# Three edits around two gathered matrix products: slots found in batches, turned tiles copied by ScalarE, stores issued by SyncE

## The chip, the core and the metric

The kernel runs on one NeuronCore of a Trainium2 chip. The metric is device time in microseconds, lower is better. Before the change the median of three runs is 1250.01 us (1247.91 to 1253.24).

## What is computed

32 images of 3x96x96 are cut into 16x16 patches, shifted and embedded (36 tokens of 192 numbers each), and 32 text tokens are fetched from a table. That gives T = 2176 tokens, 17 tiles of 128. One attention layer of 12 heads, which keeps the 32 largest scores, is added to them. What matters here is the last layer, cut to its core:

```python
x = layernorm(h)                                  # [2176, 192]
logits_fk = (x @ W_fk + b_fk) @ normed(emb_fk).T  # [2176, 128], the same for rk
w_fk, _ = topk_sparsify(softmax(logits_fk), 4)    # 4 of 128 weights stay, made to sum to 1
w_rk, _ = topk_sparsify(softmax(logits_rk), 4)
all_h = einsum('bsd,ndr->bsnr', x, f_know)        # f_know: 128 matrices of 192x128
h1 = einsum('bsnr,bsn->bsr', all_h, w_fk)
all_out = einsum('bsr,nrd->bsnd', h1, r_know)     # r_know: 128 matrices of 128x192
h = h + einsum('bsnd,bsn->bsd', all_out, w_rk)
```

Only the products with a weight are made: 4 for each token and each of the two layers.

## The kernel before

Up to 526 us the kernel embeds and attends; up to 615 us it chooses four matrices for each token (routing). Neither is touched. Then, all in f32:

- *Slots.* Each (token, matrix) pair gets a row, a slot, in a DRAM buffer in which the rows of one matrix lie together. `find_slots(r, i)` on VectorE (L1481) works the slots of tile i for layer r out in six short dependent steps, four comparisons against a list of the 128 matrices among them. For r = 0 all 17 tiles are done in a row; then the weights are made to sum to 1 (`weights_known`), and `m_xT`, which lies over the same memory as the positions of r = 0, is cleared (L1525).
- *Scatter.* GpSimd sends each tile's rows to their slots with four indirect DMAs (L692, buffer `slots_x`). The tokens are split into part 0 (tiles 0 to 8) and part 1 (9 to 16); `sent0` and `sent1` count the landed ones.
- *First product.* A part is a list of groups of 4 x 128 slots: 25 groups in part 0, 24 in part 1. 16 of each are main groups, in which every half tile of 64 slots belongs to a fixed matrix; the others are spill groups, whose matrix numbers are read at run time. Part 0 has the spill groups last, part 1 has them first. For a group SyncE loads 384 KB of rows (`load_rows`, L456), up to four groups ahead; TensorE turns each tile (L1152, a transpose into PSUM); VectorE copies the turned tile from PSUM to `m_halves` (`turned_first`, L1534); TensorE multiplies (L1166 main, L1163 spill); ScalarE copies the product from PSUM to `m_yh` (`keep_first`, L886) and issues the store of the group to `slots_h` on its own DMA queue. TensorE turns two tiles ahead of the two that it multiplies. `m_yh` has four buffers (`m_out0` to `m_out3` count their stores).
- *Sums.* When all stores of a part have landed, GpSimd fetches for each of its tiles the four product rows of each token (`fetch`, L700), VectorE finds the tile's slots of layer r = 1 and adds the rows, weighted (`first_sums`: `find_slots` and `sum_back`, L1559, L1562), and GpSimd scatters the sums into `slots_g` (`spread_sums`, L707).
- *Second product.* The same with 256 KB loads (L498), L1201 for turning, `turned_second` (L1542) for VectorE's copy, L1212 and L1210 for main and spill, `keep_second` (L903) and 384 KB stores. `r_know` (16 chunks of 768 KB) is loaded over `f_know` in part 1 of the first product, each chunk as soon as the matrices beneath it have had their last use.
- *Output.* GpSimd fetches the rows of `slots_y`, VectorE adds them and the residual (L1571), SyncE stores them (L487).

Each engine runs its own list in order. VectorE's list is written out by `beside`: all the turned copies of part 0; then those of part 1 with the nine `first_sums` of part 0 between them, one after every two or three groups; then the turned copies of the second product with the `first_sums` of part 1 and the output sums of part 0 between them. SyncE's list holds the loads, `load_r`, and later the output stores; before its first `load_rows` it waits for `slots_zeroed`, `weights_known`, `tiles_known`, issues the last three chunks of `f_know`, and waits for `sent0`.

## Time and profile before

| what | us |
|---|---|
| median of three runs | 1250.01 |
| the profiled execution | 1248.79 |
| its span, first to last instruction | 1247.0 |
| TensorE busy with matmuls | 881.7 (71%) |
| VectorE busy | 753.1 (60%) |
| GpSimd busy | 529.8 (42%) |
| ScalarE busy | 329.2 (26%) |
| mean granted TensorE clock | 0.742 of full speed |

The profile comes from one execution with the hardware profiler; its times run from the first instruction. L1152 is line 1152 of the kernel. Busy shares are means over stages of quite different limits, so the stages are read one by one. In a row, out<-in names the tiles with buffer numbers left out; some names stand for the memory they lie in: `early` holds the loaded rows and the gathered rows and sums, `place` holds `m_halves`, `m_y` also `m_yh`. "idle before <-releaser" is the engine's idle time before that instruction and what ended it, as inferred from semaphore events; "remote" is a release for which the profile shows no source.

### The profile page before, as it was taken

How to read it: one execution, taken by the hardware profiler on the slowest of the kernel's cores; microseconds unless marked ns; L12 is line 12 of the kernel's file. 1: busy time of each engine (PE TensorE's matmuls, PEld its weight loads, DVE VectorE, ACT ScalarE, POOL GpSimd, SP SyncE). 2: the span in 40 equal slices, each digit the busy share in tenths (PEclk: the TensorE clock that was granted, in tenths of full speed). 3: DMA queues.
4: the chain of work that ended last, by engine and by line, in shares of the span. 5: the costliest groups of instructions: out<-in, count | busy, mean ns of one | idle time of the engine just before them, and what ended most of it. 6: DMA issues, size and time to landing. Idle time of an engine off the chain costs nothing.

```text
span 1247.0 us, 24432 instructions
## 1 busy us (share of the span) xinstructions
PE 881.7 (71%) x6616; PEld 750.0 (60%) x6616; DVE 753.1 (60%) x4773; ACT 329.2 (26%) x1042; POOL 529.8 (42%) x745
## 2 busy tenths in 40 slices
PE   4788988898989898667400099987778656757830
PEld 4788878888888787444200088987556333633630
DVE  1399999999999999444553444334445344424533
ACT  0234433333433343144200033211111222213410
POOL 3244444444544443245376500043443544454235
PEclk9778888787878655555555599987775676878975
DMA  5123332323233330086021555444785544447833
GB/s 189 33 69 110 141 110 89 109 89 109 90 109 111 113 113 25 19 208 162 7 79 67 169 196 188 149 126 126 256 318 205 182 146 151 140 154 229 272 127 95
DMA packets 81318, 167.70 MB, mean 134 GB/s; under 512 B 12944, under 2 KB 39376, under 8 KB 79536
## 3 DMA queue, kind: packets, MB, share of 16 engines
q1 hardware_dynamic: 55824, 111.18, 27.5%
q10 hardware_dynamic: 14112, 32.12, 7.4%
q0 software_dynamic: 11264, 23.09, 6.3%
q8 instruction: 42, 0.69, 0.2%
q14 instruction: 76, 0.62, 0.2%
HBM read 84.81 MB, written 81.53 MB: 133 GB/s over the span
## 4 chain that ended last, share of the span: by engine, by line
PE 36%; DVE 32%; issue 18%; POOL 5%; DMA 4%; another core or an unknown queue 2%; ACT 2%; DVEq 1%; SPq 0%; POOLq 0%; ACTq 0%
DVE work L1301 13%; DVE top L1295 9%; PE bank L1166 6%; PE bank L1163 5%; PE bank L1212 5%; PE bank L1152 4%; PE bank L1210 3%; POOL early L700 2%; PE bank L1201 2%; PE bank L1099 1%; PE bank L925 1%; PE bank L984 1%; PE bank L1006 1%; POOL slots_g L707 1%
## 5 line engine op out<-in xcount | busy, mean ns | idle before, releaser
L1301 DVE MATCH_REPLACE8 work<-top,work 102x68 f32<-102x68 f32 x1024 | 204.7, 212 | 0.0
L1534 DVE COPY place<-bank 96x256 f32<-96x256 f32 x196 | 74.5, 416 | 149.2 <-PE bank L1152 98.3
L1295 DVE MAX8 top<-work 102x8 f32<-102x68 f32 x1024 | 145.5, 213 | 3.2 <-ACT tru L767 1.9
L1152 PE MATMUL bank<-ident,early 128*96 128x128 f32 x392 | 73.4, 316 | 102.9 <-DMA early<-slots_x 101.2
L886 ACT ACTIVATE m_y<-bank 128x128 f32<-128x128 f32 x196 | 52.5, 278 | 304.2 <-PE bank L1166 207.9
L1542 DVE COPY place<-bank 128x128 f32<-128x128 f32 x196 | 47.5, 286 | 133.0 <-PE bank L1201 73.1
L707 POOL DMA_INDIRECT slots_g<-early,s_all x68 | 66.1, 973 | 138.8 <-DVE early L1562 123.2
L1152 PEld LDWEIGHTS bank<-ident,early 128*96 128x96 f32 x392 | 52.3, 175 | 118.3 <-issue 117.9
L700 POOL DMA_INDIRECT early<-slots_h,s_all x68 | 65.2, 959 | 122.9 <-DMA slots_h<-m_y 102.5
L925 PE MATMUL bank<-xa,early 128*96 128x144 f32 x512 | 102.0, 352 | 16.8 <-DVE early L1319 16.0
L903 ACT ACTIVATE m_y<-bank 128x192 f32<-128x192 f32 x196 | 61.1, 331 | 170.5 <-PE bank L1212 78.8
L1166 PE MATMUL bank<-f_all,place 96*64 96x128 f32 x1024 | 92.6, 324 | 15.0 <-issue 11.1
L925 PEld LDWEIGHTS bank<-xa,early 128*96 128x96 f32 x512 | 91.5, 200 | 18.2 <-issue 15.9
L1212 PE MATMUL bank<-r_all,place 128*64 128x192 f32 x512 | 70.3, 400 | 40.5 <-DVE place L1542 25.6
L700 POOL DMA_INDIRECT early<-slots_y,s_all x68 | 64.7, 952 | 68.8 <-DMA slots_y<-m_y 29.9
L1166 PEld LDWEIGHTS bank<-f_all,place 96*64 96x64 f32 x1024 | 71.9, 160 | 30.2 <-issue 18.2
L1006 PE MATMUL bank<-v,pT 68*68 68x17 f32 x768 | 75.9, 250 | 14.6 <-ACT pT L792 14.6
L1006 PEld LDWEIGHTS bank<-v,pT 68*68 68x68 f32 x768 | 74.0, 196 | 17.1 <-ACT pT L792 17.1
L692 POOL DMA_INDIRECT slots_x<-early,s_all x68 | 66.0, 970 | 40.8 <-DVE s_all L1506 20.6
L1163 PE MATMUL bank<-f_all,place 96*128 x544 | 73.5, 293 | 10.5 <-ACT m_y L886 4.3
L629 POOL TENSOR_TENSOR sc<-work,tru 102x544 f32<-102x544 f32 x32 | 42.7, 1333 | 90.0 <-ACT work L805 89.9
L1301 DVE MATCH_VALUE_LOAD work<-top,work 102x8 f32 x1024 | 80.2, 78 | 0.0
(179 smaller groups left out, 1815.9 us busy)
## 6 DMA issues: line engine op xcount, KB each, us to landing
early<-slots_x SPq DMA_DIRECT2D x49, 384.0 KB
slots_y<-m_y ACTq DMA_DIRECT2D x49, 384.0 KB
slots_h<-m_y ACTq DMA_DIRECT2D x49, 256.0 KB
early<-slots_g SPq DMA_DIRECT2D x49, 256.0 KB
f_all<-in_f_know SPq DMA_DIRECT2D x16, 768.0 KB, 5.6
r_all<-in_r_know SPq DMA_DIRECT2D x16, 768.0 KB
slots_x<-zero SPq DMA_DIRECT2D x28, 360.0 KB, 3.0
slots_x<-zero SPq DMA_DIRECT2D x28, 336.0 KB, 3.2
```

The source lines that it names most:

```text
L692: nc.gpsimd.indirect_dma_start(slots_x[part_of(i)], bass.IndirectOffsetOnAxis(s_all[:, 0, i, k:k + 1], 0), xn_all[:, i, :], None).then_inc ...
L700: nc.gpsimd.indirect_dma_start(g_in[:, i % DEPTH, k, 0:width], None, src, bass.IndirectOffsetOnAxis(s_all[:, r - 1, i, k:k + 1], 0)).then_ ...
L707: nc.gpsimd.indirect_dma_start(slots_g[part_of(i)], bass.IndirectOffsetOnAxis(s_all[:, 1, i, k:k + 1], 0), g_sum[:, i % DEPTH, 0:R], None) ...
L925: nc.tensor.matmul(half, wa[:, 4 * a + c, e * HALF:(e + 1) * HALF], xa[:, :, a:a + 2 * GRID - 1:2, c:c + 2 * GRID - 1:2], start=(a == 0 an ...
L1006: last = nc.tensor.matmul(ps_pt[0:S, head * (HD + 1):(head + 1) * (HD + 1)], pT[:, g, h * S:(h + 1) * S], v[:, par, head, :], start=True, ...
L1152: last = nc.tensor.transpose(turn_bank[t][0:HALF, c * P:(c + 1) * P], m_x[:, d, t, c:D:2], ident[:])
L1163: last = nc.tensor.matmul(bank[2 + t][:, 0:R], m_xT[0:HALF, t, c, h * P:(h + 1) * P], matrix[:, c * R:(c + 1) * R], start=(h == 0 and c == ...
L1166: last = nc.tensor.matmul(bank[2 + t][h * HALVED:(h + 1) * HALVED, 0:R], m_halves[0:HALF, t, c, h, :], matrix[:, c * R:(c + 1) * R], start ...
L1212: last = nc.tensor.matmul(bank[2 + t][h * HALVED:(h + 1) * HALVED, 0:D], m_halves[:, t, 0, h, :], matrix, start=True, stop=True)
L1295: last = nc.vector.max(top8[:, c, :], work[:, par, c, :])
L1301: last = nc.vector.match_replace(work[:, par, c, :], top8[:, c, :], work[:, par, c, :], TAKEN)
L1534: nc.vector.tensor_copy(m_halves[0:HALF, t], turn_bank[t][0:HALF, 0:2 * P].rearrange("p (c h s) -> p c h s", c=2, h=2)).then_inc(sem["m_xt ...
```

## The change

`find_slots` takes a batch of tiles at a time, in four batches (1, 2, 6 and 8 tiles), and both layers are done before any product; the weights come after the second batch. The turned tiles are copied by ScalarE, two tiles ahead of the products that it keeps, and VectorE has only the sums after the slots. The stores of both products are issued by SyncE, one after each `load_rows` or `load_sums` of its loop.

```diff
+BATCHES = ((0, 1), (1, 3), (3, 9), (9, NT))
+IN_FLIGHT = 8
...
+            def store_rows(r, g, n, rows, at, copies):
+                j = FIRST_GROUP[g] + n
+                sp.wait_ge(sem[f"m_done{r}"], (j + 1) * GROUP)
+                sp.dma_start(rows[at * GROUP * P:(at + 1) * GROUP * P, :].rearrange("(p t) d -> p t d", p=P),
+                             copies[:, j % DEPTH]).then_inc(sem[f"m_out{j % DEPTH}"], 16)
...
                     if n + DEPTH < PART_GROUPS[g]:
                         load_rows(g, n + DEPTH)
+                    store_rows(0, g, n, slots_h[g], first_order(g)[n], m_yh)
                     while g == 1 and chunk < CHUNKS and n > PART_GROUPS[1] - PART_MAIN + ...
                         load_r(chunk)
...
                     if n + DEPTH < PART_GROUPS[g]:
                         load_sums(g, n + DEPTH)
+                    store_rows(1, g, n, slots_y[g], n, m_y)
...
-                pool.wait_ge(sem["slots_known0"], i + 1)
+                pool.wait_ge(sem["slots_known0"], 1 + [i < end for first, end in BATCHES].index(True))
...
             def spread_sums(i):
                 pool.wait_ge(sem["summed1"], i + 1)
+                pool.wait_ge(sem["slots_known1"], 1 + [i < end for first, end in BATCHES].index(True))
...
-            def keep_first(g, n):   (and keep_second: both wait, copy and issue the store)
+            def copy_turned(r, j, t):
+                act.wait_ge(sem[f"m_turn{r}"], j * GROUP + t + 1)
+                if j >= 1:
+                    act.wait_ge(sem[f"m_mm{r}"], (j - 1) * GROUP + t + 1)
+                if r == 0:
+                    ins = nc.scalar.activation(m_halves[0:HALF, t], turn_bank[t][0:HALF, 0:2 * P]..., ACT.Copy)
+                else:
+                    ins = nc.scalar.activation(m_halves[:, t, 0], turn_bank[t][:, 0:P]..., ACT.Copy)
+                ins.then_inc(sem[f"m_xt{r}"], 1)
+
+            def keep(r, g, n, copies, width):
+                j = FIRST_GROUP[g] + n
+                d = j % DEPTH
+                for t in range(0, GROUP, AHEAD):
+                    for ahead in range(t + AHEAD, t + 2 * AHEAD):
+                        if ahead < GROUP:
+                            copy_turned(r, j, ahead)
+                        elif n + 1 < PART_GROUPS[g]:
+                            copy_turned(r, j + 1, ahead - GROUP)
+                    if t == 0 and r * GROUPS + j >= DEPTH:
+                        act.wait_ge(sem[f"m_out{d}"], 16 * (in_turn(d, GROUPS) * r + j // DEPTH))
+                    for now in range(t, t + AHEAD):
+                        act.wait_ge(sem[f"m_mm{r}"], j * GROUP + now + 1)
+                        nc.scalar.activation(copies[:, d, now, :], bank[2 + now][:, 0:width], ACT.Copy).then_inc(sem[f"m_done{r}"], 1)
...
+                for m in range(size * K4):
+                    i, k = divmod(m, K4)
+                    if m >= IN_FLIGHT:
+                        st.wait(IN_FLIGHT - 1)
+                    st.done(nc.vector.scalar_tensor_tensor(s_hit[:, m % IN_FLIGHT], iota_e[:], ids[:, i, k:k + 1], here[:, i],
+                                                           ALU.is_equal, ALU.mult, accum_out=s_f[:, i, k:k + 1]))
...
+            find_slots(0, 0)
+            find_slots(0, 1)
+            spread_weights()
+            for n in range(2, len(BATCHES)):
+                find_slots(0, n)
             nc.vector.memset(m_xT, 0.0).then_inc(sem["halves_cleared"], 1)
+            for n in range(len(BATCHES)):
+                find_slots(1, n)
...
-            def beside(turned, g, tiles, step):   (and turned_first, turned_second)
+            for i in range(NT):
                 sum_back(1, i, R)
+            for i in range(NT):
                 sum_back(2, i, D)
```

In the batched `find_slots` the other steps stand once for the whole batch, over [128, tiles, 128] or [128, tiles, 4].

## Rows read from the trace of the kernel before

**Rows 1.** Busy time of each engine by stage.
```profile
core 0: us, PE busy (x) PEld busy (x) DVE busy (x) ACT busy (x) POOL busy (x), PEclk, DMA share, GB/s
615.00:716.00 101.00, 0.04 (x1) 0.00 (x0) 47.85 (x278) 0.00 (x0) 65.96 (x68) 0.50 0.29 95
716.00:815.00 99.00, 98.77 (x1025) 88.30 (x1026) 39.08 (x104) 28.05 (x101) 0.00 (x0) 0.98 0.56 180
815.00:966.00 151.00, 122.28 (x937) 101.21 (x935) 69.03 (x272) 24.50 (x95) 66.03 (x69) 0.75 0.61 207
...
975.00:1105.00 130.00, 87.03 (x500) 59.07 (x499) 54.32 (x260) 31.59 (x100) 57.49 (x61) 0.78 0.49 153
```

**Rows 2.** In order of time (start, length, engine, line), from scatters to first turn.
```profile
619.30 1.19 POOL L692 DMA_INDIRECT slots_x<-early,s_all  x1 [13.11 <-DVE s_all L1506]
...
664.03 0.96 POOL L692 DMA_INDIRECT slots_x<-early,s_all  x1 [0.30 <-issue]
...
703.25 1.76 DVE L1525 MEMSET place<- 128x2048 f32 x1 [0.60 <-DVE weights L1521]
704.04 25.42 SPq L456 DMA_DIRECT2D early<-slots_x  x8
...
716.23 1.93 PE L1152 MATMUL bank<-ident,early 128*96 128x128 f32 x8 [101.19 <-DMA early<-slots_x]
```

**Rows 3.** In order of time, VectorE: first step of tiles 0 and 1, a late step.
```profile
615.67 0.29 DVE L1488 SCALAR_TENSOR_TENSOR s_over<-place,base 128x128 f32<-128x128 f32 x1 [0.15 <-DVE tile_e L1475]
...
618.47 0.29 DVE L1488 SCALAR_TENSOR_TENSOR s_over<-place,base 128x128 f32<-128x128 f32 x1
...
663.67 0.16 DVE L1497 SCALAR_TENSOR_TENSOR s_i<-idf,s_f 128x4 int32<-128x4 f32 x1 [8.34 <-remote]
```

**Rows 4.** In order of time, TensorE in both products, undisturbed.
```profile
726.73 0.69 PE L1152 MATMUL bank<-ident,early 128*96 128x128 f32 x4
...
728.42 0.68 PE L1152 MATMUL bank<-ident,early 128*96 128x128 f32 x4
...
1149.09 0.44 PE L1201 MATMUL bank<-ident,early 128*128 128x128 f32 x2
...
1150.26 0.44 PE L1201 MATMUL bank<-ident,early 128*128 128x128 f32 x2
...
1188.73 1.47 PE L1210 MATMUL bank<-r_all,place 128*128 x8
```

**Rows 5.** The chain that ended last (start, length, link), spill groups of part 0.
```profile
775.24 1.79 PE bank L1163 x16
777.47 1.79 PE bank L1163 x16
```

**Rows 6.** In order of time, ScalarE: a 96x256 copy in the routing.
```profile
551.17 0.38 ACT L841 ACTIVATE t_xT<-bank 96x256 f32<-96x256 f32 x1
```

**Rows 7.** The page's costliest groups: ScalarE's copies of the products.
```profile
L886 ACT ACTIVATE m_y<-bank 128x128 f32<-128x128 f32 x196 | 52.5, 278 | 304.2 <-PE bank L1166 207.9
...
L903 ACT ACTIVATE m_y<-bank 128x192 f32<-128x192 f32 x196 | 61.1, 331 | 170.5 <-PE bank L1212 78.8
```

**Rows 8.** VectorE's turned copies (L1534, L1542), by stretches with GpSimd active: busy, count, clock, DMA.
```profile
815.40:825.40 10.00, 1.95 (x5) 1.00 0.40 120
...
905.40:915.40 10.00, 2.71 (x8) 0.95 0.92 345
...
1022.90:1032.80 9.90, 2.04 (x9) 0.79 0.37 113
...
1110.00:1126.00 16.00, 2.21 (x9) 0.71 0.57 179
```

**Rows 9.** In order of time: loads to first turn in the second product, last store.
```profile
971.90 4.34 SPq L498 DMA_DIRECT2D early<-slots_g  x5
...
974.80 1.09 PE L1201 MATMUL bank<-ident,early 128*128 128x128 f32 x4 [10.28 <-DMA early<-slots_g]
...
1196.46 0.33 ACTq L905 DMA_DIRECT2D slots_y<-m_y  x1
```

More of the change, by code:

```diff
@@ L320, in wait, with __init__, done @@
                 self.eng.wait_ge(self.sem, self.base + self.at)
+        class Tally:
+            def __init__(self, eng, name):
+                self.eng, self.sem, self.count = eng, sem[name], 0
+            def done(self, ins):
+                ins.then_inc(self.sem, 1)
+                self.count += 1
+            def wait(self, lag=0):
+                self.eng.wait_ge(self.sem, self.count - lag)
         def logits_of(i):
@@ L908, in _ @@
+            act.wait_ge(sem["m_mm0"], GROUPS * GROUP)
             for g in range(2):
-                for j in range(FIRST_GROUP[g], FIRST_GROUP[g] + PART_GROUPS[g]):
-                    keep_second(g, j)
+                for t in range(AHEAD):
+                    copy_turned(1, FIRST_GROUP[g], t)
+                for n in range(PART_GROUPS[g]):
+                    keep(1, g, n, m_y, D)
         @block.tensor
@@ L1477, in _, with find_slots @@
             nc.vector.sem_inc(sem["tiles_known"], 1)
-            slot_steps = [Steps(dve, f"slot_steps{r}", 6) for r in range(2)]
-            def find_slots(r, i):
-                st = slot_steps[r]
-                q, size = 2 * part_of(i) + r, HALVED
-                st.start(i)
-                st.done(nc.vector.scalar_tensor_tensor(s_over[:], place[:, r, i], float(size), base[:, q], ALU.is_ge, ALU.mult))
+            slot_steps = Tally(dve, "slot_steps")
+            def find_slots(r, n):
+                st = slot_steps
+                first, end = BATCHES[n]
+                size = end - first
+                here = place[:, r, first:end]
+                ids = idf[:, first:end, r]
+                starts = base[:, 2 * part_of(first) + r].unsqueeze(1).to_broadcast([P, size, NE])
+                st.done(nc.vector.scalar_tensor_tensor(s_hit[:, 0:size], here, float(HALVED), starts, ALU.is_ge, ALU.mult))
@@ L1489, in find_slots @@
                 st.wait()
-                st.done(nc.vector.tensor_tensor(s_at[:], s_over[:], place[:, r, i], ALU.add))
+                st.done(nc.vector.tensor_tensor(here, s_hit[:, 0:size], here, ALU.add))
                 st.wait()
-                for k in range(K4):
-                    last = nc.vector.scalar_tensor_tensor(s_hit[:, k, :], iota_e[:], idf[:, i, r, k:k + 1], s_at[:],
-                                                          ALU.is_equal, ALU.mult, accum_out=s_f[:, k:k + 1])
@@ L1495, in find_slots @@
-                st.done(last)
+                for m in range(size * K4):
[4 more added lines that the diff above has]
+                                                           ALU.is_equal, ALU.mult, accum_out=s_f[:, i, k:k + 1]))
                 st.wait()
-                st.done(nc.vector.scalar_tensor_tensor(s_i[:, 0], idf[:, i, r], float(size), s_f[:], ALU.mult, ALU.add))
+                at = [s_i[:, step, 0:size] for step in range(4)]
@@ L1571, in sum_back @@
                     nc.vector.tensor_tensor(g_sum[:, d, :], g_sum[:, d, :], t_h[:, i % 2, :], ALU.add).then_inc(sem["summed2"], 1)
-            def first_sums(i):
-                find_slots(1, i)
+            for i in range(NT):
                 sum_back(1, i, R)
-            def beside(turned, g, tiles, step):
-                done = 0
-                for n in range(PART_GROUPS[g]):
-                    turned(FIRST_GROUP[g] + n)
-                    while done < len(tiles) and (done + 1) * PART_GROUPS[g] <= (n + 1) * len(tiles):
-                        step(tiles[done])
-                        done += 1
-                assert done == len(tiles)
-            def output(i):
-                sum_back(2, i, D)
-            for n in range(PART_GROUPS[0]):
-                turned_first(n)
-            beside(turned_first, 1, range(*PARTS[0]), first_sums)
-            dve.wait_ge(sem["m_mm0"], GROUPS * GROUP)
-            beside(turned_second, 0, range(*PARTS[1]), first_sums)
-            beside(turned_second, 1, range(*PARTS[0]), output)
-            for i in range(*PARTS[1]):
-                output(i)
+            for i in range(NT):
+                sum_back(2, i, D)
 _INS = ["a_x", "l_x", "text_ids", "w_shift_a", "w_shift_l", "w_mid_a", "w_mid_l", "tok_vec", "tok_bias", "vocab",
```

89 lines of the change are left out of this document (29 added, 60 removed).

## The prediction

> **What bounds the kernel now.** I read the busy time by stage first, then the start of the dispatch in order of time, then the rhythm of the two products with and without GpSimd beside them. The changed code runs after 615 us; what lies before it is untouched. The stages [rows 1] say three things. From 615 to 716 TensorE does nothing. In the first product's part 0 (716 to 815) it is busy throughout at clock 0.98. In part 1 (815 to 966) and in the second product's part 0 (975 to 1105) the same kind of work takes 151 and 130 us instead of 99, at clock 0.75 and 0.78. Part 1 of the second product follows from 1111 to 1196, then a tail.
>
> Why TensorE waits until 716: GpSimd's scatters run from 619.30, and the 36th, the last of part 0, is issued at 664.03 [rows 2]; part 0 is therefore in DRAM near 667. SyncE loads the first rows at 704.04 all the same, because it first waits for the weights, which VectorE computes after the slots of all 17 tiles. One tile's slots take 2.80 us (615.67 to 618.47), so 17 would be ready at 663; but from 637 on steps of VectorE that only wait for the step before begin up to 8.34 us late [rows 3], and it comes to the clearing of m_xT, which follows the weights, only at 703.25 [rows 2].
>
> Undisturbed, two tiles of the first product recur every 1.69 us on single-matrix groups [rows 4], 3.38 a group of four tiles, and every 2.23 on spill groups [rows 5], 4.46 a group. In the second product it is 1.17 a pair, 2.34 a group, and 1.5 a pair, 3.0 a spill group [rows 4]. By that, part 1 would be 16 x 3.38 + 8 x 4.46 = 90 us, not 151; the second product's part 0 16 x 2.34 + 9 x 3.0 = 64, not 130. What is missing there: VectorE's slots and sums stand between the turned copies, TensorE stalls, its clock falls.
>
> **The change, part by part.**
>
> *Slots in batches.* Tile 0 alone costs the same 2.8 us, and GpSimd starts at 619.3 as before. Of its 2.8 us the four comparisons are 1.1, and in a batch only they repeat for each tile: two tiles then cost about 4 us, the weights 2, six tiles about 10. GpSimd, at 1.27 us a scatter ((664.03 - 619.30) / 35), has work all along. The weights are known near 625, so the three late chunks of f_know no longer stand ahead of the rows. The last batch of eight starts near 634 and needs 12.5 us without stalls. The late steps fall into it, but it has some eight serial steps and a window of eight comparisons where the tiles had over forty serial steps. I take 10 us more: 657, with the clearing of m_xT (1.76 us [rows 2]) 659. The event that comes last is then the part-0 scatter at 667. The first load follows it, and 3 us later the first turn (971.90 to 974.80 is such a start [rows 9]): 671 instead of 716.2. Gain 45 us; if VectorE ended near 701 as now, only the f_know chunks ahead of the load would go, and it would be 10 or so.
>
> *Copies on ScalarE.* A 96x256 PSUM copy is seen on it at 0.38 us, its stores at 0.278 and 0.331 [rows 6, 7]. A pair is 2 x 0.38 + 2 x 0.28 = 1.3 us of the 1.69 that TensorE needs, in the second product 2 x 0.28 + 2 x 0.33 = 1.2 of 1.17 to 1.5. Issued back to back they overlap a little, so I cost this at nothing, hidden by TensorE's own pace; without the overlap it is 0.05 us for each of 64 single-matrix pairs of the second product, 3 us. Queued behind each wait for m_out are now the next turned copies; four buffers, over 9 us, cover a store.
>
> *Stores on SyncE.* 98 issues of 0.33 us [rows 9] beside groups of 2.3 us and more: hidden. But the loads of the next part now stand behind the last store of this part. In the first product that is new: TensorE waits one load, 3 us [rows 9]. In the second the bubble exists already.
>
> *GpSimd beside the products.* This decides the size. Whenever GpSimd has issued DMAs for a few microseconds, all engines get their signals late. Nine windows of GpSimd activity in the first product hold 60 turned copies in 85 us, from x5 to x8 in 10 us: 5.7 us a group. Eight in the second hold 62 in 74 us: 4.8 a group. In one unbroken run (1110 to 1126) there are x9 in 16 us: 7.1 a group [rows 8]. The change takes the slots and sums out of the copies' way, but it also lets GpSimd issue without pause. So the bounds for a group beside GpSimd are 2.3 to 4.5 us (no effect once the copies are alone) and 7.1. I take 5.7 and 4.8, the many windows rather than the one.
>
> *The sum.*
> - First product, part 0: GpSimd scatters until 619.3 + 68 x 1.27 = 706; those 35 us give 6 groups. The other 19 are 10 x 3.38 + 9 x 4.46 = 74. 671 + 35 + 74 = 780.
> - Part 1 starts at 783. GpSimd's 72 DMAs are 91 us, with their start 94: 16.5 groups by 877. The last 7.5 share the DMA with r_know: 393 + 262 KB of rows and 1.33 chunks of 786 KB are 1.7 MB a group, at 345 GB/s and share 0.92 [rows 8] less GpSimd's part 5.0 us. 38 us: 915.
> - Second product from 918. GpSimd's 64 DMAs take 83 us: 17 groups; 8 spill groups at 3.0 are 24. 1025, with the load 1028.
> - Part 1 of it: 36 fetches, 45 us, 9 groups; 7 x 2.34 + 8 x 3.0 = 40. 1113.
> - Tail as now: 1247.0 - 1196.5 [rows 9] = 50.5. Span 1163.5; the profiled execution lies 1.8 above its span: 1165. The median of the runs shown is 1.2 above that execution; I leave that out.
>
> **The rivals.**
>
> *Signals are prompt once VectorE is out of the copies* (1100). For: part 0 of the first product runs at full pace with the same matmuls. Against: the 9 copies in 16 us happened while VectorE did hardly anything else. Then the parts are 671 + 94 + 3 + (36 + 74) + 3 + 84 (GpSimd's 83 is now longer than TensorE's 64) + 3 + 62 + 50.5 + 1.8: 1082. I add 18 for a clock that falls in the DMA-bound stretch: 1100.
>
> *Serial copies under late signals* (1210). ScalarE now has four waits a pair in one line (two turned tiles, two products), where two engines shared them. If each is late, a group beside GpSimd takes 7 to 8 us. At 7.5: 5 groups in 35 us, 12.5 in 94, 11 in 83, 6 in 45; the others at undisturbed pace add 77, 58, 39 and 48. 671 + 112 + 3 + 152 + 3 + 122 + 3 + 93 + 50.5 + 1.8 = 1211. It holds if the long run [rows 8] is the rule. VectorE's start staying at 701 adds 30 to the forecast, 1195, and is counted here.
>
> *One queue for everything* (slower, 1310). The stores join a queue in which row loads and 16 chunks of 786 KB stand. If a store lands later than four groups, ScalarE waits on m_out and the turned copies behind it wait too, so TensorE stops once a group. I take a load's 2.9 us [rows 9] for a store's landing; exposed on half of the 98 groups that is 142 us on top of 1165. It decides from a backlog of about four groups, 9 to 13 us, 3 to 4 MB at 300 GB/s. Against it: only SyncE's own pace fills the queue, and it stops for each group. The Trainium skill (DMA: Bandwidth & Descriptors, Queues, rings and completion order) says that each DMA engine takes turns between queue rows by packets; by that a store on ScalarE's row had a turn of its own, and now has none. The same page (Issuing engines are not separate DMA queues) says that issuing from several engines saves only the time to issue. By the second rule the sum stands, by the first this rival gains weight; no row here tells them apart.
>
> *The change isn't felt*: the scatters, not VectorE, would set each step. GpSimd is busy 66 us of 151 in part 1 [rows 1], so I see no reason.
>
> **How the numbers follow.** Forecast 0.47, prompt signals 0.19, serial copies 0.26, one queue 0.05, not felt 0.03. Range 1090 to 1225, which takes in all but the last two and the ends of their neighbours. A measurement tells 0.5% (6 us) from no change. Faster 0.92, same 0.02, slower 0.06: part of the last two cases is slower, and a few of the serial ones.
>
> **What would show it.** First rows loaded near 667 and first turn near 671; weights near 625. No find_slots or sum between turned copies; TensorE waiting for ScalarE and not VectorE. Copies per 10 us beside GpSimd: 7 to 8 is the forecast, 10 or more the first rival, 5 the second. ScalarE's keep waiting on a DMA of the stores would show the third. GpSimd's spreads, which now wait 7 us for each sum, should wait less than 3. The prediction is wrong if the first turn comes after 690, or if part 1 of the first product takes under 115 or over 150 us.

## The result, and the profile after

The changed kernel is slower: 1310.30 us median of four runs (1306.37 to 1312.12), against 1251.62 (1247.91 to 1267.62) for the kernel before, measured beside it. The ratio is 1.0475, 95% interval 1.0434 to 1.0516 (ratios are of the means of the runs, without the few, here the one of 1267.62, that lie over 1.5% above the fastest of their kernel). Forecast was 1165, with 1225 as the upper end: the sign is wrong. The profiled execution took 1312.12, its span is 1310.3, its clock 0.72.

The changed kernel by stages (columns as in [rows 1]): up to the first turn, the rest of GpSimd's scatters, then in turn a stretch without and one with GpSimd.

```profile
core 0: us, PE busy (x) PEld busy (x) DVE busy (x) ACT busy (x) POOL busy (x), PEclk, DMA share, GB/s
619.00:677.00 58.00, 2.73 (x16) 2.35 (x17) 54.69 (x316) 1.51 (x4) 45.50 (x42) 0.50 0.42 132
677.00:719.00 42.00, 11.81 (x76) 7.99 (x72) 1.02 (x7) 3.78 (x15) 25.64 (x27) 0.58 0.28 96
719.00:819.00 100.00, 95.91 (x915) 84.15 (x913) 0.00 (x0) 54.76 (x182) 0.90 (x1) 0.89 0.45 146
819.00:916.00 97.00, 22.51 (x102) 17.75 (x102) 12.29 (x36) 5.47 (x16) 68.78 (x72) 0.54 0.23 69
916.00:1009.00 93.00, 86.88 (x858) 74.86 (x858) 0.00 (x0) 52.37 (x176) 0.00 (x0) 0.89 0.74 275
1009.00:1099.00 90.00, 14.66 (x74) 6.62 (x74) 10.96 (x32) 7.07 (x26) 61.89 (x64) 0.54 0.27 81
1099.00:1163.00 64.00, 58.49 (x428) 44.76 (x429) 0.00 (x0) 43.91 (x175) 0.89 (x1) 0.95 0.68 224
```

Read the PE and POOL columns together: 915 matmuls in the 100 us without GpSimd, 102 in the 97 with it. TensorE, ScalarE and VectorE all nearly stop; only GpSimd goes on, at 72 DMAs in 97 us. In order of time within such a stretch, TensorE with one DMA of GpSimd and one copy of ScalarE (start, length, engine, line; in brackets its idle time before, and what ended it):

```profile
865.91 0.37 PE L1193 MATMUL bank<-f_all,place 96*128 x1 [1.73 <-issue]
...
867.81 0.94 POOL L722 DMA_INDIRECT early<-slots_h,s_all  x1 [0.30 <-issue]
868.01 0.37 PE L1182 MATMUL bank<-ident,early 128*96 128x128 f32 x1 [1.73 <-issue]
...
870.81 0.37 PE L1182 MATMUL bank<-ident,early 128*96 128x128 f32 x1 [2.43 <-issue]
...
874.31 0.37 PE L1182 MATMUL bank<-ident,early 128*96 128x128 f32 x1 [3.13 <-issue]
...
876.48 0.28 ACT L927 ACTIVATE m_y<-bank 128x128 f32<-128x128 f32 x1 [22.07 <-remote]
...
877.81 0.37 PE L1182 MATMUL bank<-ident,early 128*96 128x128 f32 x1 [3.13 <-issue]
```

The four of L1182 are the turns of one group, and the profile names no wait before them: "issue". The starts lie 2.10, 2.80, 3.50 and 3.50 us apart, whole multiples of 0.70. A matmul itself is not slow (0.37 us). TensorE's `issue` before L1193 (51.7 us) and, but for 1.3 us, before L1242 (54.8) and all of ScalarE's 139.8 us `remote` before L927 fall into the stretches with GpSimd.

In the kernel before the same stretch looked otherwise. GpSimd's waits of 810 to 1120 us in the kernel before, run again in another set:

```profile
POOL slots_g L707 <- DVE early L1562: 126.1, 17, 11.9
```

and those of the changed kernel, 815 to 1100 us:

```profile
POOL slots_g L730 <- issue: 20.8, 68, 0.4
```

Before, GpSimd waited for a sum before each tile's spreads, 17 times, 7.4 us on average; now the 68 spreads only follow the 0.3 us between one issue and the next. Its issuing has become one unbroken run of 72 and one of 64 DMAs.

### The profile page after: what moved, and what is told of

Its sections match the earlier page's. It is cut to its first block, busy times and chain, and to the rows that moved or that the text cites. A ratio compares the mean times of both kernels' runs of the same rounds, so it can differ in the third digit from the quotient of the medians.

```text
span 1310.3 us, 24240 instructions
## 1 busy us (share of the span) xinstructions
PE 867.3 (66%) x6616; PEld 741.6 (57%) x6616; DVE 603.4 (46%) x4173; ACT 431.2 (33%) x1434; POOL 535.7 (41%) x745
## 3 DMA queue, kind: packets, MB, share of 16 engines
q0 software_dynamic: 11264, 23.09, 5.9%
## 4 chain that ended last, share of the span: by engine, by line
PE 34%; DVE 26%; issue 21%; another core or an unknown queue 8%; POOL 5%; DMA 3%; ACT 2%; DVEq 0%; SPq 0%; POOLq 0%; ACTq 0%
DVE work L1331 12%; DVE top L1325 8%; PE bank L1196 6%; PE bank L1193 5%; PE bank L1182 5%; PE bank L1242 4%; PE bank L1240 3%; PE bank L1231 2%; POOL early L722 2%; DMA early<-slots_x 2%; PE bank L955 1%; PE bank L1129 1%; PE bank L1036 1%; PE bank L1113 1%
## 5 line engine op out<-in xcount | busy, mean ns | idle before, releaser
L1581 DVE TENSOR_SCALAR early<-early,weights 128x128 f32<-128x128 f32 (+1 forms) x34 | 10.7, 314 | 506.7 <-issue 269.9
L927 ACT ACTIVATE m_y<-bank 128x128 f32<-128x128 f32 (+1 forms) x392 | 116.9, 306 | 290.0 <-remote 139.8
L1242 PE MATMUL bank<-r_all,place 128*64 128x192 f32 x512 | 66.8, 384 | 100.8 <-issue 54.8
L1182 PE MATMUL bank<-ident,early 128*96 128x128 f32 x392 | 73.8, 314 | 80.3 <-DMA early<-slots_x 66.9
L1193 PE MATMUL bank<-f_all,place 96*128 x544 | 76.3, 292 | 64.3 <-issue 51.7
L1193 PEld LDWEIGHTS bank<-f_all,place 96*128 96x128 f32 x544 | 70.6, 206 | 67.2 <-issue 67.1
L1182 PEld LDWEIGHTS bank<-ident,early 128*96 128x96 f32 x392 | 51.6, 174 | 98.0 <-issue 89.4
L1196 PE MATMUL bank<-f_all,place 96*64 96x128 f32 x1024 | 87.7, 315 | 29.0 <-issue 29.0
L908 ACT ACTIVATE place<-bank 96x256 f32<-96x256 f32 x196 | 66.1, 377 | 117.1 <-PE bank L1182 80.5
L1242 PEld LDWEIGHTS bank<-r_all,place 128*64 128x64 f32 x512 | 34.2, 154 | 121.5 <-issue 77.2
L1196 PEld LDWEIGHTS bank<-f_all,place 96*64 96x64 f32 x1024 | 68.9, 155 | 41.6 <-issue 34.5
L714 POOL DMA_INDIRECT slots_x<-early,s_all x68 | 71.4, 1050 | 33.5 <-issue 20.4
```

The lines of the kernel that those rows point to most:

```text
L714: nc.gpsimd.indirect_dma_start(slots_x[part_of(i)], bass.IndirectOffsetOnAxis(s_all[:, 0, i, k:k + 1], 0), xn_all[:, i, :], None).then_inc ...
L908: ins = nc.scalar.activation(m_halves[0:HALF, t], turn_bank[t][0:HALF, 0:2 * P].rearrange("p (c h s) -> p c h s", c=2, h=2), ACT.Copy)
L927: nc.scalar.activation(copies[:, d, now, :], bank[2 + now][:, 0:width], ACT.Copy).then_inc(sem[f"m_done{r}"], 1)
L1182: last = nc.tensor.transpose(turn_bank[t][0:HALF, c * P:(c + 1) * P], m_x[:, d, t, c:D:2], ident[:])
L1193: last = nc.tensor.matmul(bank[2 + t][:, 0:R], m_xT[0:HALF, t, c, h * P:(h + 1) * P], matrix[:, c * R:(c + 1) * R], start=(h == 0 and c == ...
L1196: last = nc.tensor.matmul(bank[2 + t][h * HALVED:(h + 1) * HALVED, 0:R], m_halves[0:HALF, t, c, h, :], matrix[:, c * R:(c + 1) * R], start ...
```

## The experiments

Each set of runs has its own runs of the kernel before, and they are not alike: 1251.62 in the set of the result, 1258.16, 1274.20 and 1269.00 us in three more, but 1120.48 and 1131.99 in two others, one of these on the very chip that gave 1269.00. In these two no kernel below shows the standstill. I call these two sets calm. Ratios are taken within a set.

**Both kernels unaltered, again**, beside the measurements below:

> The changed kernel once more, unaltered, on the chip of this call. The kernel before took 1250 to 1258 us on two occasions and 1120 once, beside the first two measurements, so the standstill of the engines beside GpSimd's DMAs may hang on the chip or the placing and not on the kernel alone. Theory: where the kernel before takes near 1250, the changed one takes near 1310; where it takes near 1120, there is no standstill, and the changed kernel is faster, 1060 to 1110. Rival: the ratio of the two is the same everywhere, 1.04 to 1.05, and the changed kernel takes near 1170 where the other takes 1120.

> The kernel before, unaltered, for its trace on this chip. Theory: if its time is near 1120, VectorE's slots end near 665 and not 701, and part 1 of the first product takes about 110 us and not 151. If it is near 1250, the trace is as shown.

The changed kernel took 1313.26 us (1310.48 to 1315.2), ratio 1.0322 [1.0273, 1.037] to 1274.20; the kernel before, as one of the kernels of that set, 1260.73. TensorE stands in the changed one again, 20 matmuls in 20 us where the kernel before has 107:

```profile
830.00:850.00 20.00, 5.80 (x20) 3.94 (x18) 2.36 (x8) 0.66 (x2) 15.28 (x16) 0.50 0.18 52
```

```profile
830.00:850.00 20.00, 17.55 (x107) 16.02 (x108) 8.35 (x33) 3.00 (x12) 7.74 (x8) 0.76 0.36 100
```

**Stores back on ScalarE.** The queue of SyncE is as it was; the rest of the change stays.

```diff
-                    store_rows(0, g, n, slots_h[g], first_order(g)[n], m_yh)
...
+                act.wait_ge(sem[f"m_done{r}"], (j + 1) * GROUP)
+                act.dma_start(rows[...], copies[:, d]).then_inc(sem[f"m_out{d}"], 16)
```

> The changed kernel with the stores of both products back on ScalarE's queue, each after the last of its group's copies. Theory (GpSimd's unbroken issue): within 1% of the changed kernel, 1300 to 1320. Rival B (one queue): most of the loss goes, 1200 to 1250. Rival A (ScalarE's list is the bound): a little slower still, 1320 to 1340, as ScalarE's list grows by 98 issues of 0.33 us and waits for its own copies.

1306.68 us (1303.41 to 1312.86), ratio 1.0442 [1.0342, 1.0542]. The stores' place makes no difference here, and the rival of the one queue falls. TensorE beside GpSimd (830 to 850 us) stands as in the changed kernel:

```profile
830.00:850.00 20.00, 3.94 (x13) 2.60 (x11) 2.70 (x8) 0.38 (x1) 15.12 (x17) 0.50 0.17 51
```

The Trainium skill (DMA: Bandwidth & Descriptors, Issuing engines are not separate DMA queues) says that issuing from several engines saves issue time alone; the runs agree, at 1306.68 and 1310.30 us.

**Turned copies back on VectorE**, its sums between them as before; slots in batches and stores on SyncE stay.

```diff
-            for i in range(NT):
-                sum_back(1, i, R)
+            beside(turned_first, 1, range(*PARTS[0]), lambda i: sum_back(1, i, R))
...
+            beside(turned_second, 1, range(*PARTS[0]), lambda i: sum_back(2, i, D))
```

> The changed kernel with the turned copies back on VectorE and the sums between them in the order of before; slots in batches and stores on SyncE stay. The sums hold GpSimd back again, so it pauses after every eight DMAs. Theory (GpSimd's unbroken issue): the products take what they took before, the start 40 us less less the crawl beside the rest of the scatters: 1195 to 1230. Rival A (ScalarE's serial list): the same, 1190 to 1230; this run alone doesn't tell these two apart, the paced one does. Rival B (one queue): as slow as the changed kernel, about 1300.

1235.04 us (1231.56 to 1242.47), ratio 0.9836 [0.9746, 0.9926], 5 us above the upper end of what was expected. One part taken back turns a loss of 4.8% into a gain of 1.6%. With the sums again between the copies, GpSimd waits for them, 17 times for 107.7 us. The same stretch:

```profile
830.00:850.00 20.00, 17.29 (x140) 16.86 (x141) 7.11 (x19) 4.00 (x16) 7.71 (x8) 0.93 0.43 135
```

It does not tell ScalarE's copies from the pauses of GpSimd. The next does.

**Paced.** The changed kernel whole, but GpSimd waits for the products' counters before each block of four DMAs. The scatters of part 1, but for the first tile, wait too, for three groups of the first product per tile.

```diff
+                if i > PARTS[1][0]:
+                    pool.wait_ge(sem["m_mm0"], 3 * (i - PARTS[1][0]) * GROUP)
...
+            def keep_pace(r, g, block, blocks):
+                if block > 0:
+                    pool.wait_ge(sem[f"m_mm{r}"], (FIRST_GROUP[g] + block * PART_GROUPS[g] // blocks) * GROUP)
...
+                        keep_pace(*during, 2 * (i - first) + 1, 2 * (end - first))
```

> The changed kernel with one thing added: GpSimd does its DMAs beside the products in blocks of four, and waits before each block until TensorE has done its share of the part's groups. Nothing else differs. Theory (GpSimd issuing indirect DMAs without a pause starves the other engines of instructions; the change took the pauses away): the four stretches in which TensorE nearly stands still (from about 680, 826, 1020 and 1172 us) go, and the time falls from 1310 to between 1120 and 1190 us. Rival A (four waits in ScalarE's one list are the cost): the pauses change little, 1280 to 1310. Rival B (stores and loads in SyncE's one queue): also 1280 to 1310.

1168.27 us (1163.85 to 1174.79), ratio 0.9310 [0.9218, 0.9402], against 1258.16 in the same set. It beats both kernels; the changed one, in other sets, is 142 to 145 us slower. ScalarE's copies, the batches and SyncE's stores are all in it; only the pauses are new.

```profile
830.00:850.00 20.00, 15.43 (x159) 13.37 (x157) 1.81 (x6) 8.34 (x31) 10.97 (x12) 1.00 0.53 168
```

12 DMAs in 20 us instead of 17, and 159 matmuls where the changed kernel has 15.

**Narrow rows.** The same DMA instructions beside the products, with rows of 64 bytes (the sums are of these 16 values, the rest is left out).

```diff
-                    nc.gpsimd.indirect_dma_start(g_in[:, i % DEPTH, k, 0:width], None, src,
+                    nc.gpsimd.indirect_dma_start(g_in[:, i % DEPTH, k, 0:16], None, src.rearrange("n (a b) -> (n a) b", b=16),
```

> The changed kernel with the same number of fetches and spreads by GpSimd after the first scatters, each of 128 rows of 64 bytes in place of 512 or 768; the rest of each row isn't moved. Theory in the form that the act of issuing does it: TensorE crawls as much as in the changed kernel, 1290 to 1320. Rival in the form that the bytes or the packets' time in the DMA engines do it: the crawl shrinks with the bytes, under 1220.

1311.76 us, one run. The software queue moved 9.16 MB instead of 23.09, and nothing changed: 12 matmuls from 830 to 850. The bytes are not what does it.

**A measurement by itself.** TensorE runs 241 matmuls, ScalarE and VectorE 241 small copies each, without any wait between them, four times: beside nothing, beside 64 unbroken indirect stores of GpSimd, beside 64 plain ones of GpSimd, beside 64 of SyncE. The output is zeros. The profile has two records for each of these matmuls, 1928 for the 964 of the program, so 92 in 10 us, the full pace, are 46 matmuls, and 241 take 52 us.

```diff
+            for n in range(N):
+                nc.gpsimd.indirect_dma_start(rows, bass.IndirectOffsetOnAxis(idx[:, n:n + 1], 0), src[:], None).then_inc(sem["landed"], 16)
```

First in the calm set of 1120.48:

> Not the computation: only a measurement, the output is zeros. Four phases, in each TensorE runs 240 matmuls of 128x128, ScalarE 240 copies and VectorE 240 copies of 64 columns, all written out one by one and with no wait between them. Phase 1: no DMA. Phase 2: GpSimd issues 64 indirect scatters of 96 KB without a pause. Phase 3: 64 plain DMAs from GpSimd. Phase 4: 64 plain DMAs from SyncE. Theory (instructions of the other engines come late whatever they wait for): in phase 2, from about 10 us on, single instructions start at multiples of 0.7 us, and 240 matmuls take well over 100 us instead of 65; phases 1 and 4 are undisturbed. Rival (only the signals between engines are late): phase 2 runs like phase 1.

264.26 us, and nothing crawled: no answer. Then, unaltered, in the set of 1274.20:

> The measurement without waits again, on the chip of this call. It ran undisturbed in the call in which the kernel before took 1120 us. Theory (the chip or placing decides): where the kernel before takes near 1250, phase 2 shows single matmuls at multiples of 0.7 us. Rival: undisturbed again, since nothing in it waits.

313.55 us. Its second stretch, from before GpSimd's first DMA to after its last:

```profile
55.00:60.00 5.00, 4.85 (x44) 4.66 (x43) 2.60 (x20) 2.60 (x18) 2.04 (x2) 1.00 0.06 20
60.00:65.00 5.00, 4.06 (x37) 3.89 (x36) 4.29 (x33) 4.48 (x30) 3.78 (x5) 1.00 0.23 79
65.00:70.00 5.00, 2.24 (x6) 1.33 (x7) 1.99 (x12) 2.26 (x12) 3.78 (x5) 0.63 0.24 82
...
90.00:100.00 10.00, 1.12 (x3) 1.15 (x4) 1.57 (x7) 1.79 (x7) 7.56 (x9) 0.50 0.22 78
...
140.00:145.00 5.00, 0.74 (x2) 0.58 (x2) 1.00 (x5) 1.13 (x5) 0.00 (x0) 0.50 0.00 0
145.00:150.00 5.00, 2.66 (x12) 2.85 (x13) 2.88 (x21) 2.97 (x19) 0.00 (x0) 0.50 0.00 0
150.00:155.00 5.00, 5.00 (x40) 5.00 (x39) 5.00 (x40) 5.00 (x35) 0.00 (x0) 0.83 0.02 3
```

GpSimd's first DMA starts at 57.66. For 6 us nothing happens; then the other three engines crawl until 147.7, 9 us after the last DMA ended. In order of time within the crawl:

```profile
91.00 0.26 ACT L152 ACTIVATE a_to<-one 128x64 f32<-128x64 f32 x1 [1.14 <-issue]
91.00 0.23 DVE L164 COPY d_to<-bank 128x64 f32<-128x64 f32 x1 [1.18 <-issue]
91.71 0.37 PE L142 MATMUL bank<-one 128*128 128x128 f32 x1 [2.43 <-issue]
92.02 0.96 POOL L105 DMA_INDIRECT rows<-src,idx  x1 [0.30 <-issue]
92.40 0.26 ACT L152 ACTIVATE a_to<-one 128x64 f32<-128x64 f32 x1 [1.14 <-issue]
92.40 0.23 DVE L164 COPY d_to<-bank 128x64 f32<-128x64 f32 x1 [1.18 <-issue]
93.11 0.29 PEld L142 LDWEIGHTS bank<-one 128*128 128x128 f32 x1 [2.51 <-issue]
```

No engine waits for another here, and yet ScalarE and VectorE start together, every 1.40 us, and TensorE gets one weight load or matmul in 1.40. The page's row of tenths (40 slices) shows all four stretches, first of this run:

```profile
PE   7999999952111101111999999999999999999970
...
POOL 1000000477777777760000001999920000000000
```

then of the same kernel in the calm set (span 262.5 instead of 311.8 us):

```profile
PE   7999999999999999910004999999999999999940
...
POOL 1000000007777777777776999970000000000000
```

(TensorE's 0s there are the end of its second stretch, where it has finished and waits for GpSimd's last landing.) Plain DMAs of GpSimd, the 9s of its row, and those of SyncE in the last stretch disturb nobody in either. GpSimd's DMAs cost it the same 0.963 us in both. A version of the measurement in which TensorE and ScalarE wait for each other went the same way in this set:

> Only a measurement, the output is zeros. As the first of this kind, but TensorE and ScalarE hand a tile to each other 100 times in each phase, and VectorE waits for each of its own 100 copies. Phase 1 no DMA, 2 indirect scatters without a pause, 3 plain DMAs from GpSimd, 4 from SyncE. Theory in the form that waits are needed: on a chip where the changed kernel takes near 1310, phase 2 slows to steps of multiples of 0.7 us. Rival (instructions without waits are held up too): then the measurement without waits is slow as well on this chip.

It crawls at the same pace (4 matmuls in 10 us), so waits add nothing of their own, and the run without waits shows that they are not needed for it. The whole takes 257.92 us, less than the other because each stretch has 101 matmuls of the program and not 241.

A version in which TensorE loops over ten matmuls, so that it brings in no new instructions, met calm sets twice:

```diff
-                straight(pe, 240, lambda m: nc.tensor.matmul(...))
+                looped(pe, 240, lambda m: nc.tensor.matmul(...))
```

> The same measurement with TensorE's 240 matmuls as a loop of 24 rounds over 10 matmuls; the other engines as in the first. Theory in the form that fetching the instructions is what is slow: TensorE runs at full pace in phase 2, as the loop's body is at hand, while ScalarE and VectorE still crawl. Rival (the sequencers themselves or their queues are held up): TensorE crawls in the loop too.

> Only a measurement, output zeros: as the straight one, but TensorE runs its 240 matmuls as a loop of 24 rounds of 10, so that it need not bring new instructions in from memory, while ScalarE and VectorE stay straight. Second stretch: GpSimd issues 64 indirect stores without a pause. Theory (the engines' issue is held up, whatever they run): TensorE in the loop starts under 4 matmuls in 10 us, as without a loop. Rival (instructions arrive late from memory): the loop runs at full pace (33 or more in 10 us) while the straight copies crawl.

262.62 and 264.70 us, full pace throughout (92 matmuls in 10 us beside the unbroken run). Whether fetching or issuing is held up stays open. One trace bears on it, the changed kernel's in the set of 1269.00. VectorE is late there from 667 on, 10 instructions in the 8.6 us before TensorE's first turn. TensorE, which had waited 58.5 us for its rows, then runs at full pace beside it:

```profile
673.60:679.00 5.40, 5.36 (x42) 4.44 (x42) 1.36 (x3) 1.50 (x4) 3.93 (x5) 0.63 0.95 349
```

and crawls only after those 42 matmuls and 42 weight loads, with 7 matmuls in the 10 us from 679. That fits instructions that were at hand before the wait ended and come late afterwards, better than a hold on all starts alike. It is an observation, no experiment.

**Pauses, and rows.** The same measurement with other stretches: 64 indirect stores in blocks of four with waits for the landing, 64 unbroken ones of 32 rows instead of 128, 64 unbroken ones of 128 rows.

```diff
+                if n % 4 == 3:
+                    pool.wait_ge(sem["landed"], 16 * (n + 1))
...
+                nc.gpsimd.indirect_dma_start(rows, bass.IndirectOffsetOnAxis(idx[0:32, n:n + 1], 0), src[0:32, :], None).then_inc(sem["landed"], 16)
```

> Only a measurement: 241 matmuls (TensorE), 241 copies each (ScalarE, VectorE) without any wait between them, four times; the output is zeros, nothing of the reference is computed. The first time GpSimd rests; the second it issues 64 indirect stores of 128 rows in blocks of 4, each block waiting for its landing; the third 64 unbroken of 32 rows; the fourth 64 unbroken of 128 rows (the control). Theory (issue without a pause builds up something that is worked off at one instruction in 0.70 us): the second stretch is undisturbed (28 to 32 us for TensorE's 241), the fourth crawls about 5 us after the first DMA (TensorE starts under 3 matmuls in 10 us), and the third tells whether it goes by instructions (crawls as the fourth) or by rows (undisturbed, or a crawl that comes later). Rival (whenever an indirect DMA is under way the others are slow): the second stretch crawls in proportion, over 60 us. If the fourth doesn't crawl either, this chip doesn't show the effect and nothing is learnt.

That met a calm set (339.00 us, every stretch at full pace) and told nothing. Again:

> Only a measurement, output zeros: 241 matmuls and copies without waits, four times: beside nothing, beside 64 indirect stores in blocks of 4 with waits for the landing (pauses of 1.6 to 3.6 us each 6.4 to 8 us), beside 64 unbroken ones of 32 rows, beside 64 unbroken ones of 128 rows. Where before is 1115 to 1140 all four run at full pace (92 matmuls in 10 us), as measured. Where before is 1245 to 1275: theory, the fourth crawls (under 5 matmuls in 10 us from about 6 us after the first DMA on), the second does not or less; the third tells whether it goes by instructions (crawls) or by rows (does not, or later).

446.48 us.

Ten microseconds of each stretch of it, in this order:

```profile
80.00:90.00 10.00, 9.00 (x80) 8.96 (x79) 8.82 (x67) 9.25 (x63) 5.99 (x7) 1.00 0.21 71
...
190.00:200.00 10.00, 1.11 (x3) 1.15 (x4) 1.57 (x7) 1.79 (x7) 7.56 (x9) 0.50 0.09 24
...
330.00:340.00 10.00, 1.49 (x4) 0.86 (x3) 1.57 (x7) 1.79 (x7) 7.56 (x9) 0.50 0.23 78
```

80 matmuls beside the blocks (92 is full pace), 3 and 4 beside the unbroken runs. With a quarter of the rows it is as bad: it goes by DMA instructions. The blocks start a DMA each 1.6 us on average (58.7 to 159.7 for 64), the unbroken runs each 1.17 (32 rows) and 1.27 (128 rows).

**Short pauses in the kernel.** After each DMA of a fetch or a spread GpSimd clears a 128x512 tile and waits for that.

```diff
+            def rest():
+                nc.gpsimd.memset(idle[:], 0.0).then_inc(sem["pool_steps"], 1)
+                rests[0] += 1
+                pool.wait_ge(sem["pool_steps"], rests[0])
```

> The changed kernel with a memset and a wait for it after each fetch and each spread. Where the standstill is not there it is bound by GpSimd (measured: 1164 where before is 1132). Where before is 1245 to 1275: theory (pauses of about 1 us heal it) 1160 to 1200; rival A (only a longer rest, or the tie to the products, heals it) 1290 to 1320; in between, it heals in part.

1201.38 us (1194.46 to 1204.24), ratio 0.9462 [0.9376, 0.9548], at the upper end of the theory's 1160 to 1200 and by 1.4 us beyond it; the changed kernel unaltered, in the same set, 1313.53 (1307.52 to 1319.11), ratio 1.0352 [1.0256, 1.0447]. GpSimd now starts a DMA each 1.78 us, and TensorE beside it is at full pace in the first product:

```profile
850.00:870.00 20.00, 20.00 (x241) 16.28 (x238) 1.34 (x4) 13.42 (x48) 16.66 (x24) 1.00 0.93 318
```

(the 24 are GpSimd's DMAs and clearings together). No tie to the products is needed, then; 0.8 us between the end of a DMA and the start of the next are enough. What keeps it behind the paced kernel is seen too: GpSimd takes 1.4 times as long for its DMAs, and TensorE waits for it after each part, and the scatters, which have no pauses, still hold it up at 680 to 700 (3 matmuls).

**In a calm set.** The kernel with short pauses and the paced one, before at 1131.99:

> The changed kernel whose GpSimd waits for the products' counters before each block of 4 DMAs, again, on the chip of these measurements. Theory: 1155 to 1185 where before is 1250 to 1275, as measured already, and no stretch of 20 us between 690 and 910 with under 8 us of matmuls. Rival (the first result was that chip's): over 1220.

> The changed kernel with GpSimd writing a 128x512 tile and waiting for it after each fetch and each spread (short rests, no tie to the products). Theory (pauses alone heal it, since what has piled up is worked off): 1160 to 1220 us where before is 1250 to 1275. Rival A (only standing back from the products heals it, as in the paced kernel): near the changed kernel, 1290 to 1320. Rival B (a rest of under 1 us is too short): in between, 1230 to 1290, with stretches of under 5 us of matmuls in 20.

The paced kernel: 1103.83 us (1097.09 to 1109.25), ratio 0.9781 [0.9707, 0.9854]. With short pauses: 1164.42 (1158.55 to 1173.5), ratio 1.0328 [1.0238, 1.0417]. The latter had met the other calm set before, at 1162.61 against 1120.48, one run of each:

> The changed kernel with a clearing of 512 columns on GpSimd (0.3 to 0.6 us) and a wait for it after each of its fetches and spreads beside the products and in the tail, so the issue goes on without a long pause but at 1.7 to 2.0 us a DMA instead of 1.27. Theory in the form that the rate of issue does it: at the lower rate TensorE no longer stands still, and the kernel comes near 1220 in spite of some 100 us more of GpSimd's own time. Rival in the form that any unbroken activity of GpSimd holds the others up: still slower than the changed kernel, 1330 or more.

So pauses are no gain in themselves: where nothing stands still, the kernel with the clearings is 3 to 4% slower than before, bound by GpSimd; where it does, it is 5% faster. The changed kernel itself was never run in a calm set:

> The changed kernel itself, unaltered. Theory (the loss is the standstill, which some chips show and some do not; where before takes about 1130 us they do not): if before takes 1115 to 1140 here, the changed kernel takes 1085 to 1115 and no stretch of 20 us between 690 and 910 has under 5 us of matmuls while groups remain; if before takes 1245 to 1275 here, it takes 1300 to 1320. Rival (the change loses time by something else too, which every chip shows): over 1150 where before is 1115 to 1140.

That set was not calm, and it answered 1313.53, the second branch. What the change is worth in a calm one stays open; the paced kernel's 0.978 bears on it only indirectly.

## Why the prediction was wrong

The stages, forecast and measured. Each is counted from its first turn to the next one's, the last part to its last store.

| stage | forecast | measured | difference |
|---|---|---|---|
| first turn | 671 | 674.3 | +3.3 |
| first product, part 0 | 112 | 144.7 | +32.7 |
| first product, part 1 | 135 | 193.6 | +58.6 |
| second product, part 0 | 110 | 150.2 | +40.2 |
| second product, part 1 | 85 | 97.1 | +12.1 |
| tail | 50.5 | 50.4 | -0.1 |
| span | 1163.5 | 1310.3 | +146.8 |

*Slots in batches: right.* The weights' last step is at 623.12 (forecast 625), m_xT is cleared at 646.2 instead of 703.25 [rows 2], the first load is issued at 670.98 and the first turn starts at 674.27, not 716.23. 42 of the 45 us came. VectorE's late steps did not return: in the 58 us of 619 to 677 it was busy 54.69. That was in part luck. The prediction gave fewer serial steps as the reason why they would cost only 10 us; the trace shows another difference, in GpSimd's pace. From 619 to 665 its scatters start every 1.40 us on average instead of 1.28, as some are longer beside VectorE's large instructions (2.78 us beside the clearing of m_xT, 2.00 and 1.55 beside steps of 128x1024, instead of 0.96). That also put the last scatter of part 0 at 668.64 instead of 664.03, and the first turn 3.3 us later than forecast. The other traces with this stretch, calm sets aside, go by the same pace: at 1.40 to 1.42 us (three experiments and the narrow rows) VectorE is busy 9.4 to 9.9 us from 665 to 675, at 1.395 us (short pauses) 6.65, at 1.38 us (both repeats of the changed kernel) 2.69 and 1.70. A late VectorE also lengthens fewer scatters, so which is the cause is not shown.

*Copies on ScalarE: right.* Where GpSimd rests, 86 turned copies took 93 us in the first product (912 to 1005, beside the r_know chunks) and 62 us in the second (1098 to 1160), that is 4.3 and 2.9 us a group; the sum had 3.4 to 5.0 and 2.3 to 3.0. At 0.377 and 0.28 us each the copies cost what was taken for them.

*Stores on SyncE: right.* The last store of part 0 is issued at 815.22, and the next turn starts at 818.97. TensorE's stop is named for the load and lasts 4.09 us, forecast 3:

```profile
806.75 8.79 SPq L481 DMA_DIRECT2D slots_h<-m_y  x3
815.64 5.64 SPq L469 DMA_DIRECT2D early<-slots_x  x5
...
818.97 1.95 PE L1182 MATMUL bank<-ident,early 128*96 128x128 f32 x8 [4.09 <-DMA early<-slots_x]
```

*GpSimd beside the products: wrong, and all of the loss is here.* The step read: "So the bounds for a group beside GpSimd are 2.3 to 4.5 us (no effect once the copies are alone) and 7.1. I take 5.7 and 4.8, the many windows rather than the one." The changed kernel's turned copies in GpSimd's stretches, first product (L908), then second (L910), columns as in [rows 8]:

```profile
677.00:710.00 33.00, 0.76 (x2) 0.60 0.29 99
819.00:912.00 93.00, 3.80 (x10) 0.54 0.24 72
...
1013.00:1098.00 85.00, 3.56 (x14) 0.54 0.24 73
...
1163.00:1197.00 34.00, 3.54 (x16) 0.60 0.44 133
```

Ten copies in 93 us are 2.5 groups, 37 us a group; 14 in 85 are 24 us; 16 in 34 are 8.5. Forecast were 16.5 groups where there are 2.5; the sign given for the forecast was 7 to 8 copies in 10 us, and there is 1. The differences of the table are those stretches' groups, done afterwards: 14 groups at 4.3 us are 60 us, and part 1 of the first product took 58.6 more (193.6 in all, where the prediction called itself wrong from 150 on). (The value of 5.7 was itself misread: the nine windows hold 62 copies, not 60, so 5.5 us a group; over 94 us that is half a group, 2 to 3 us.)

Two things went wrong in that step. The windows of [rows 8] were windows of the kernel before, in which GpSimd stops for each sum: blocks of eight DMAs, 10 us, and then 7 us of rest. A slow start that takes 6 us and more to set in and about 10 to pass can't show its depth in them; they are a mean over both. The prediction itself said that the change "also lets GpSimd issue without pause", and then took the value measured with pauses. The one row without a pause (x9 in 16 us) was set aside as one against many, though of all windows of the copies it alone had the condition that the change makes permanent. Nor was its 7.1 an upper bound: 8 of the 9 copies and 44 matmuls lie in its first 9 us, one and 4 in its last 7. And the scatters, 36 in a row, were a longer unbroken run, whose late steps [rows 3] the prediction used for the start and not for the price. These are the end of the one and the depth of the other, from the kernel before (columns as in [rows 1]):

```profile
1119.00:1126.00 7.00, 0.91 (x4) 0.30 (x4) 0.29 (x1) 0.66 (x2) 5.48 (x6) 0.76 0.40 128
...
655.00:665.00 10.00, 0.00 (x0) 0.00 (x0) 0.28 (x3) 0.00 (x0) 7.69 (x8) 0.50 0.23 79
```

Secondly, the mechanism was held to be late signals. It holds up instructions that wait for nothing, so there was no reason why fewer waits should help, and none why it should stay at microseconds a group.

*The rivals.* "Prompt signals" said 1100, which nothing reached but the paced kernel in a calm set, at 1103.83, where the kernel before is at 1131.99 too. "Serial copies" had the right place and not the mechanism: waits of ScalarE, at 7.5 us a group, and 1210. "One queue" forecast the right number, 1310, by a mechanism that the stores put back on ScalarE refute: ratio 1.0442 against 1.0475 with them on SyncE. No case in the prediction had GpSimd's own pauses as what kept the others going.

The cause, as far as it is shown: with pauses and everything else kept, 1168.27; with unbroken issue, 1306.68 to 1313.53 in four sets; by itself, without a kernel around it, 3 to 4 matmuls in 10 us instead of 92. The Trainium skill (SBUF — State Buffer, SBUF: two separate sides) says that compute and DMA cannot slow each other at the memory, and knows one trap, where VectorE keeps GpSimd from writing its descriptors. The traces agree that no instruction of the others became longer: ScalarE's longest copy of the measurement took 258 ns where it crawls and 257 ns in the calm set. Scatters that are longer beside VectorE's instructions are seen as well (2.78 us instead of 0.96), though in the kernel before those beside the same clearing stayed at 0.96. The standstill goes the other way round, from GpSimd's issuing to the starts of the others.

Not shown: what is shared. It could be how instructions reach the engines, for which the 42 matmuls above speak, or a path on which GpSimd's indirect DMAs and the engines' starts are both told of. All executions here were recorded by the profiler, so no run tells whether the recording has a part in it. And nothing here says why two sets are calm.

## What to carry to other kernels

A rate measured beside an engine that pauses holds only while it pauses: before an engine is set free, ask which of its waits the others lived on, and take the price from the longest stretch without such a wait, without its first microseconds. Where GpSimd issues indirect DMAs beside other work, keep them on average at 1.6 us each or more, best in blocks of about four with a wait on the progress of that work between them; here it turned 4.8% more into 6.9% less. And where matmuls that wait for nothing start in even steps far apart, look at what another engine issues, not at their own operands.

## What the runs showed of the hardware

- Unbroken indirect DMAs of GpSimd, one in 1.17 to 1.27 us, in the sets that are not calm, hold TensorE, ScalarE and VectorE to starts at multiples of 0.70 us, to 9 or 10 us after the last. It sets in some 6 us after the first in the measurement alone and 9 to 19 us after it in the kernels. One in 1.6 us with pauses left 80 matmuls of 92, one in 1.78 us all of them. Without pauses but at one in 1.40 us VectorE was not held up for 46 us (busy 54.69 of the 58 us from 619); at one in 1.38 it was late after as long, in two traces. That speaks for the rate and not the pause as such, but no run varied the rate alone between 1.27 and 1.6.
- It goes by instructions: a quarter of the rows, or 9.16 MB instead of 23.09, changed nothing. Plain DMAs of GpSimd at 0.54 us each, and SyncE's, did nothing of the kind.
- It comes and goes with the set of runs, on one and the same chip (before at 1131.99 and 1269.00). In the calm ones the kernel before is 10 to 12% faster.
- The granted clock followed: 0.54 of full speed in the two long stretches where TensorE stood, that is near its lower level, 1.2 GHz, and 0.89 to 0.95 in those between.
